# A two-stage classifier contraction: the transposed operand made by crossbar DMAs instead of GpSimd products

## What is computed

```
variables = [softmax(p) for p in split(logits, 4, axis=-1)]     # four of 512 x 16: v0, v1, v2, v3
joint = outer product of the four, per row b                    # 512 x 16 x 16 x 16 x 16
flat = joint.reshape(512, 65536)
num_y_joint = einsum('bj,by->yj', flat, y_true)
num_joint = sum(flat, axis=0)
prob = clip(max(num_y_joint, 1e-6) / max(num_joint, 1e-6), 0, 1)
probs = einsum('yj,bj->by', prob, flat)                         # 512 x 100
```

## Time and profile before

| | |
|---|---|
| device time, median of 3 runs (lowest, highest) | 584.12 us (584.08, 584.28) |
| span of the profiled execution | 582.4 us |
| median less that span | 1.7 us |
| TensorE busy | 539.0 us, 93% |
| VectorE busy | 345.8 us, 59% |
| GpSimd busy | 135.8 us, 23% |
| ScalarE busy | 55.7 us, 10% |
| moved by DMA | 4.57 MB |

### The profile page before, as it was taken

One profiled execution on the slowest core, in us unless ns is written; L12 is line 12 of the kernel. 1 busy time (PEld: TensorE's weight loads), 2 busy tenths in 40 slices (PEclk: granted clock), 3 DMA queues, 4 the chain that ended last, 5 costly groups with the idle time before them and its releaser, 6 DMA issues.

```text
span 582.4 us, 10067 instructions
## 1 busy us (share of the span) xinstructions
PE 539.0 (93%) x3088; PEld 302.5 (52%) x3088; DVE 345.8 (59%) x735; ACT 55.7 (10%) x119; POOL 135.8 (23%) x96
## 2 busy tenths in 40 slices
PE   4777887579999999999999999999999999999996
PEld 2343443235555555555555555555555555555553
DVE  7899999996673644444454644445354644445445
ACT  4445454000001000000001000000001000000000
POOL 4899999990001300000001300000001300000000
PEclk9999998988999999999999999999999999999999
DMA  2111110000000000000000000000000000000000
GB/s 75 42 54 37 54 36 0 0 0 0 0 0 1 1 0 0 0 0 0 0 0 0 0 0 0 0 0 0 0 0 0 0 0 1 0 0 0 0 0 14
DMA packets 3013, 4.57 MB, mean 8 GB/s; under 512 B 816, under 2 KB 1072, under 8 KB 3008
## 3 DMA queue, kind: packets, MB, share of 16 engines
q1 hardware_dynamic: 2480, 4.30, 2.3%
q10 hardware_dynamic: 528, 0.20, 0.1%
HBM read 4.27 MB, written 0.24 MB: 8 GB/s over the span
## 4 chain that ended last, share of the span: by engine, by line
PE 77%; DVE 16%; issue 4%; DVEq 1%; ACT 1%; DMA 0%; POOL 0%; ACTq 0%; POOLq 0%
PE numbers L442 13%; PE numbers L443 13%; PE numbers L444 13%; PE joined L452 12%; PE joined L454 12%; PE joined L453 12%; DVE p_lo L351 9%; DVE r_hi L371 2%; DVE ratio L366 2%; DVEq L351 1%; DVE acc L406 1%; DVE inv L364 1%; ACT p_hi L281 0%; DVE qf L188 0%; DVE den L361 0%
## 5 line engine op out<-in xcount | busy, mean ns | idle before, releaser
L442 PE MATMUL numbers<-q_hi,p_hi 128*128 128x404 f16 (+1 forms) x508 | 172.7, 340 | 22.2 <-DVE p_lo L351 22.2
L452 PE MATMUL joined<-r_hi,pt_hi 128*128 128x400 f16 x512 | 170.9, 334 | 7.8 <-DVE r_lo L373 7.7
L443 PE MATMUL numbers<-q_lo,p_hi 128*128 128x404 f16 (+1 forms) x508 | 171.9, 338 | 0.0
L444 PE MATMUL numbers<-q_hi,p_lo 128*128 128x404 f16 (+1 forms) x508 | 171.8, 338 | 0.0
L453 PE MATMUL joined<-r_lo,pt_hi 128*128 128x400 f16 x512 | 170.7, 333 | 0.0
L454 PE MATMUL joined<-r_hi,pt_lo 128*128 128x400 f16 x512 | 170.5, 333 | 0.0
L361 DVE TENSOR_SCALAR den<-numbers 128x4 f32<-128x4 f32 x128 | 20.5, 160 | 211.2 <-PE numbers L444 209.9
L373 DVE SCALAR_TENSOR_TENSOR r_lo<-ratio,r_hi 128x400 f16<-128x400 f32 x128 | 99.5, 778 | 4.4
L442 PEld LDWEIGHTS numbers<-q_hi,p_hi 128*128 (+1 forms) x508 | 50.0, 98 | 63.7 <-issue 28.0
L258 POOL TENSOR_TENSOR qg<-qf,v0f 128x1600 f32<-128x1600 f32 x3 | 8.6, 2862 | 303.6 <-ACT qf L313 303.6
L452 PEld LDWEIGHTS joined<-r_hi,pt_hi 128*128 (+1 forms) x512 | 50.0, 98 | 50.4 <-issue 14.3
(11 more groups left out here) (53 smaller groups left out, 115.2 us busy)
## 6 DMA issues: line engine op xcount, KB each, us to landing
v1b<-v_rows SPq DMA_DIRECT2D x15, 256.0 KB, 3.2
labels<-in_r_y_true_dram ACTq DMA_DIRECT2D x1, 200.0 KB, 2.9
out_dram<-acc SPq DMA_DIRECT2D x1, 200.0 KB, 2.0
x<-in_r_logits_dram SPq DMA_DIRECT2D x1, 128.0 KB, 2.2
v_rows<-v1t SPq DMA_DIRECT2D x1, 32.0 KB, 1.6
```

What stands on the lines that cost most here:

```text
L442: pe.matmul(out, hi, qh, start=(k == 0), stop=False)
L443: pe.matmul(out, hi, ql, start=False, stop=False)
L444: last = pe.matmul(out, lo, qh, start=False, stop=(k == KC - 1))
L452: pe.matmul(out, hi, r_hi[:, slot, :], start=first, stop=False)
```

## The change

pt_hi and pt_lo are no longer computed from a transposed p23. They are copies of p_hi and p_lo whose 128 x 128 blocks are transposed on the way by `dma_start_transpose` on SP's queue, an instruction for hi and one for lo: one tile each for tiles 0 and 1, then two tiles (256 KB) for each value from 1 on. Four semaphores take turns, so that SP issues value i only when value i - 4 has landed. Removed are v1's way over DRAM, v1b, p23t, ptf, the identity matrix, all fp32 transposes of TensorE and the PSUM bank `spare`, ScalarE's copies of these, its pt_hi, and GpSimd's ptf and pt_lo. ScalarE's loop is now p_hi alone. GpSimd now begins q of groups 1 to 3 when all of p_lo is made (`p_ready` at TILES). On TensorE group 0's loop is written out value by value, since it waits on the four semaphores in turn. The unchanged parts are groups 1 to 3 and VectorE's program.

SP's queue:

```diff
-            sp.wait_ge(v1_copied, 1)
-            sp.dma_start(v1_dram, v1t[:, :]).then_inc(v1_stored, 16)
-            sp.wait_ge(v1_stored, 16)
-            for i in range(1, V1_BUFS):
-                sp.dma_start(v1b[:, i, :], v1_dram[i:i + 1, :].broadcast_to([LANES, ROWS])).then_inc(v1_spread[i], 16)
-
-            sp.wait_ge(ptf_made, 2)
-            sp.dma_start(v1b[:, 0, :],
-                         v1_dram[V1_BUFS:V1_BUFS + 1, :].broadcast_to([LANES, ROWS])).then_inc(v1_spread[0], 16)
-            def refill(i, buf):
-
-                sp.wait_ge(ptf_made, 2 * i + 2 * (1 - V1_BUFS))
-                sp.dma_start(v1b[:, buf, :],
-                             v1_dram[bass.ds(i, 1), :].broadcast_to([LANES, ROWS])).then_inc(v1_spread[buf], 16)
-
-            with sp.Fori(V1_BUFS, S - 2 * V1_BUFS + 1, V1_BUFS) as i:
-                for j in range(1, V1_BUFS + 1):
-                    refill(i + j, j % V1_BUFS)
-            for i in range(S - V1_BUFS + 1, S):
-                refill(i, i % V1_BUFS)
+            def turn(out, src, tile, tiles):
+                return sp.dma_start_transpose(
+                    out[:, bass.ds(tile * TW, tiles * TW)].rearrange("p (c b) -> p c b", b=LANES),
+                    src[:, bass.ds(tile * TW, tiles * TW)])
+
+            for h in range(2):
+                sp.wait_ge(p_hi_made, h + 1)
+                turn(pt_hi, p_hi, h, 1).then_inc(pt_hi_first[h], 16)
+                sp.wait_ge(p_ready, h + 1)
+                turn(pt_lo, p_lo, h, 1).then_inc(pt_lo_first[h], 16)
+
+            def turn_value(i, lap, j):
+
+                if lap is not None:
+                    sp.wait_ge(pt_landed[j], lap * 32)
+                sp.wait_ge(p_hi_made, 2 * i + 2)
+                turn(pt_hi, p_hi, 2 * i, 2).then_inc(pt_landed[j], 16)
+                sp.wait_ge(p_ready, 2 * i + 2)
+                turn(pt_lo, p_lo, 2 * i, 2).then_inc(pt_landed[j], 16)
+
+            for i in range(1, S):
+                turn_value(i, i // TURN_SEMS - (i % TURN_SEMS == 0) if i > TURN_SEMS else None, i % TURN_SEMS)
             sp.wait_ge(added, KC * AG)
```

GpSimd:

```diff
-            def make_pt(tile, half, buf, fill):
-
-                if half == 0 and fill is not None:
-                    pool.wait_ge(v1_spread[buf], fill)
-                if fill is not None:
-
-                    pool.wait_ge(pt_ready, tile - 1)
-                pool.tensor_tensor(ptf[:, half, :], p23t[:, half, :], v1b[:, buf, :], ALU.mult).then_inc(ptf_made, 1)
-
-            def finish_pt(tile, half):
-                pool.wait_ge(pt_hi_made, tile + 1)
-                pool.tensor_tensor(pt_lo[:, bass.ds(tile * TW, TW)], ptf[:, half, :],
-                                   pt_hi[:, bass.ds(tile * TW, TW)], ALU.subtract).then_inc(pt_ready, 1)
-
-            def make_value(i, buf, fill):
-                make_pt(2 * i, 0, buf, fill)
-                make_pt(2 * i + 1, 1, buf, fill)
-                finish_pt(2 * i, 0)
-                finish_pt(2 * i + 1, 1)
-
-
-            pool.wait_ge(v1_first_copied, 1)
-            pool.wait_ge(p23t_made, 1)
-            make_pt(0, 0, 0, None)
-            finish_pt(0, 0)
-            pool.wait_ge(p23t_made, 2)
-            make_pt(1, 1, 0, None)
-            finish_pt(1, 1)
-            for i in range(1, V1_BUFS):
-                make_value(i, i, 16)
-            with pool.Fori(V1_BUFS, S - V1_BUFS + 1, V1_BUFS) as i:
-                make_value(i, 0, i * (16 // V1_BUFS))
-                for j in range(1, V1_BUFS):
-                    make_value(i + j, j, (i + V1_BUFS) * (16 // V1_BUFS))
-
-
+            pool.wait_ge(p_ready, TILES)
```

ScalarE:

```diff
-            def make_pt_hi(tile, half):
-                act.wait_ge(ptf_made, tile + 1)
-                act.activation(pt_hi[:, bass.ds(tile * TW, TW)], ptf[:, half, :], ACT.Copy).then_inc(pt_hi_made, 1)
-
             act.wait_ge(p23_made, 1)
             make_p_hi(0, 0, 1)
             act.wait_ge(q0_right, 1)
             act.activation(q_hi[:, QH:QW], qf[:, QH:QW], ACT.Copy).then_inc(q0_right_hi, 1)
-            act.wait_ge(v1_turned, 1)
-            act.activation(v1t[:, :], v1_psum[0:S, 0:ROWS], ACT.Copy).then_inc(v1_copied, 1)
             act.wait_ge(p23_made, 2)
             make_p_hi(0, 1, 2)
-            act.wait_ge(v1_first_made, 1)
-            act.activation(v1b[:, 0, :], v1_first[:, 0:ROWS], ACT.Copy).then_inc(v1_first_copied, 1)
-            for h in range(2):
-                act.wait_ge(p23_turned, h + 1)
-                act.activation(p23t[:, h, :], turned[h][:, 0:ROWS], ACT.Copy).then_inc(p23t_made, 1)
-            make_pt_hi(0, 0)
             with act.Fori(1, S) as i:
                 make_p_hi(i, 0, 2)
-                make_pt_hi(2 * i - 1, 1)
-                make_pt_hi(2 * i, 0)
-            make_pt_hi(TILES - 1, 1)
```

TensorE (besides the transposes at the start, which are deleted):

```diff
-            pe.wait_ge(pt_ready, 1)
-            pe.wait_ge(v1_first_copied, 1)
-            pe.wait_ge(v1_copied, 1)
+            pe.wait_ge(pt_hi_first[0], 16)
+            pe.wait_ge(pt_lo_first[0], 16)
             join(0, 0, 0, first=True)
 
-            def middle(g, end, make=False):
+            def middle(g, end):
 
                 with pe.Fori(1, end) as i:
-                    if make:
-
-                        pe.wait_ge(p_ready, 2 * i + 2)
                     count(g, 2 * i, 0)
-                    if make:
-                        pe.wait_ge(pt_ready, 2 * i)
                     join(g, 2 * i - 1, 1)
                     count(g, 2 * i + 1, 1)
-                    if make:
-                        pe.wait_ge(pt_ready, 2 * i + 1)
                     join(g, 2 * i, 0)
+
+            def first_value(i, j, lap):
+
+                pe.wait_ge(p_ready, 2 * i + 2)
+                count(0, 2 * i, 0)
+                if j is None:
+                    pe.wait_ge(pt_hi_first[1], 16)
+                    pe.wait_ge(pt_lo_first[1], 16)
+                join(0, 2 * i - 1, 1)
+                count(0, 2 * i + 1, 1)
+                pe.wait_ge(pt_landed[i % TURN_SEMS], lap * 32)
+                join(0, 2 * i, 0)
...
-            middle(0, S, make=True)
-            pe.wait_ge(pt_ready, TILES)
+            first_value(1, None, 1)
+            for i in range(2, S):
+                first_value(i, i % TURN_SEMS, i // TURN_SEMS + (i % TURN_SEMS > 0))
```

More of the change, by code:

```diff
@@ L63, in sem @@
             return ctx.enter_context(nc.semaphore(name))
-        v1_dram = nc.dram_tensor("v1_rows", [S, ROWS], FP32, kind="Internal").ap()
         x = sb("x", [LANES, KC * NV, S], FP32)
@@ L72, in joint_classifier @@
         labels = sb("labels", [LANES, KC, CW], FP32)
-        ident = sb("ident", [LANES, LANES], FP32)
         p23 = sb("p23", [LANES, KC, 2 * HALF], FP32)
[L76 to L80, removed]
+        TURN_SEMS = 4
         p_hi = sb("p_hi", [LANES, TILES * TW], FP16)
@@ L103, in joint_classifier @@
         joined = [pb(f"joined{i}", [LANES, 512], FP32) for i in range(KC)]
[L104 to L108, removed]
         logits_in = sem("logits_in")
@@ L112, in joint_classifier @@
         ones_set = sem("ones_set")
-        ident_set = sem("ident_set")
         acc_set = sem("acc_set")
@@ L118, in joint_classifier @@
         soft = sem("soft")
[L119 to L124, removed]
         p23_made = sem("p23_made")
-        p23_turned = sem("p23_turned")
-        p23t_made = sem("p23t_made")
         q0_left = sem("q0_left")
@@ L137, in joint_classifier @@
         p_ready = sem("p_ready")
-        ptf_made = sem("ptf_made")
-        pt_hi_made = sem("pt_hi_made")
-        pt_ready = sem("pt_ready")
+        pt_hi_first = [sem(f"pt_hi_first{h}") for h in range(2)]
+        pt_lo_first = [sem(f"pt_lo_first{h}") for h in range(2)]
+        pt_landed = [sem(f"pt_landed{j}") for j in range(TURN_SEMS)]
         numbers_ready = sem("numbers_ready")
@@ L192, in _ @@
             pool.memset(labels[:, :, CLASSES:CW], 1.0).then_inc(ones_set, 1)
[L193 to L196, removed]
             pool.memset(acc[:, :, :], 0.0).then_inc(acc_set, 1)
@@ L411, in _ @@
         def _(pe):
[L412 to L420, removed]
-            last.then_inc(v1_first_made, 1)
-            def turn_p23(h):
-                pe.wait_ge(p23_made, h + 1)
-                for k in range(KC):
-                    last = pe.transpose(turned[h][:, k * LANES:(k + 1) * LANES],
-                                        p23[:, k, h * HALF:(h + 1) * HALF], ident[:, :])
-                last.then_inc(p23_turned, 1)
             def count_parts(g, tile, k):
@@ L467, in _ @@
             out = numbers[0][:, 0:NW]
-            turn_p23(0)
             pe.wait_ge(p_hi_made, 1)
@@ L473, in _ @@
                 if k == KC // 2:
-                    turn_p23(1)
                     pe.wait_ge(q0_right_hi, 1)
```

## The result

The changed kernel takes 548.34 us (median of 4 runs, 547.58 to 548.90), the kernel before 584.10 us on the same chip (4 runs); the ratio is 0.940, 95% interval 0.938 to 0.942. The forecast was 548.5 us. The profiled execution took 547.58 us and spans 545.8 us, where the sum gave 546.8 us.

A forecast was written before the change was run, and what follows sets the result against it. TensorE was taken to bound the kernel, except in group 0, where it waits for VectorE, held up by GpSimd. Span 582.4 - 40.6 + 1 + 4 = 546.8 us, 548.5 us as timed; range 542 to 610 us.

The forecast's parts named there:

- the sum: Whole span: profiled 582.4 us less 40.6, plus 1 and plus 4, gives 546.8 us of span, 548.5 us as timed.
- Two regimes, GpSimd the cause: Group 0: a value takes 12.42 us early, 8.17 us late; VectorE's instructions wait for gaps between GpSimd's.
- The rival that VectorE would stay slow: Group 0: p_lo slow for another reason, such as transposes' SBUF traffic; about 12 us a value, 580 to 590 us; chance 0.02.
- -40.6 us: Count 0 to count 20: GpSimd's 64 products leave group 0, so the loss of 40.6 us goes.
- The start, +1 us: Start: fp32 turns and ScalarE copies go; TensorE's clock may rise one count later, 0 to 2 us, taken as +1.
- q, +4 us: GpSimd's q of groups 1 to 3, after the last p_lo, delays VectorE's r_hi and r_lo: +4 us, bounds 0 and 6.
- The straight code, 0: TensorE's fifteen values written out: more program fetching, taken as 0; +10 us if half a dozen fetches showed.
- The transposes, hidden: Group 0: SP's two 256 KB transposes a value finish within 8.17 us and cost 0; chance 0.70, 548.5 us.
- the bound from below: Transposes in group 0: 0.52 MB a value at the SP queue's 0.32 MB/us take 1.6 us.
- The slower rival: Transposes bound group 0, costing (T - 8.17) x 15 more, T a value's two transposes; up to 810 us; chance 0.23.
- the upper bound: Transposes in group 0: blocks go one behind another, 16 at 1.6 us, 25.6 us a value, 810 us in all.

The follow-up runs named there:

- the run with the groups apart: Changed kernel with GpSimd's q of groups 2 and 3 moved apart, each made from the middle of the running group, nothing added: 547.07 us.
- both q edits: Changed kernel with GpSimd's q instructions of groups 1 to 3 cut into four and q of groups 2 and 3 moved apart: 544.00 us, ratio 0.933.
- q cut: Changed kernel with each of GpSimd's nine instructions for q of groups 1 to 3 cut into four, same place and order: 545.95 us, ratio 0.935.

## Why the prediction was right

- **Two regimes, GpSimd the cause.** Right, and shown by the run with GpSimd's work put back: a value takes 11.4 to 12.8 us again, with every other part of the change in place and nobody waiting for GpSimd. The total, 582.4 us against 583.4 us before, is as close as it is by chance: 7.3 us of it stand at the start, and the kernel before lost 14.3 us beside q instead. The rival that VectorE would stay slow is refuted by 1.67 us for four p_lo under transposes, and under four times as many.
- **-40.6 us.** Count 20 ended 40.45 us earlier. From count 0 to count 20 are 79.95 us where 39 pieces gave 79.6 us. The prediction puts the whole 40.6 us down to the products' leaving. By the starts of den, 25.9 us were lost beside the products and 14.3 us beside q, and these are gone because q now waits for the last p_lo: with q early again the time is 15.7 us longer.
- **The start, +1 us.** Count 0 ended at 15.50 us, 0.17 us earlier than before, and the clock rose at about 15.4 us: nothing was lost in this execution. In others something was (last section), inside the bounds of 0 to 2 us.
- **q, +4 us.** The number is right and its working is not, which is luck. The excess of the steps from 132.21 to 168.90 us is 4.03 us, but only 2.40 us of it stand beside q. The other 1.63 us stand beside the first sum, which follows right behind q now and has no term in the prediction; in the kernel before it stood alone, at 187.65 us, and cost 0.18 us. The step beside q was put at 5.26 us, less 2 us of slack; it is 4.4 to 4.7 us, 5.3 us only beside the first sum, and the slack does not help, as the run with the groups apart shows.
- **The straight code, 0.** TensorE is busy in all of 28 to 95 us, which is straight code.
- **The transposes, hidden.** Right in sign, with the bound from below too low: I had 1.6 us a value from the refills' 0.32 MB/us, and it is 2.8 us, by the most that SP issued and the engines moved, 184 GB/s. The landing, 3.2 us, was taken rightly from the refill. The Trainium skill (Advanced Engine Details and Errata, X-Bar Transpose) expects 350 to 400 GB/s; no run here shows it: the most is half of that, with the engines' busy share at 1.0 and SP's queue never idle. The verdict did not hang on it: 8.17 us were there for either.
- **The slower rival** was a real one, and what decides it is the number of instructions, not of blocks: 2 a value are 2.5 us of SP, 16 are 20.4 us. It would have been slower by SP's issue, not by blocks that go one behind another, as the upper bound had it. I had taken the case of large transposes for the reason that they look like refills; the better reason would have been that the cost of issue is paid once for each.

## To carry to other kernels

An engine at 23% busy can cost another its time: where a VectorE instruction lasts much longer in one stretch than in another, look at what GpSimd runs beside it, and cut GpSimd's instructions short if they cannot be moved. Before moving work to DMA transposes, count both the instructions by their issue time and the bytes by the engines' busy share, against the time of one loop; here 2.5 and 2.9 us (0.36 of 8.17 us) against 8.2 us. Slack before a wait is not a store: 2 us stood free in each step of VectorE, and a chain of 4.5 us or more in a step of 4.08 us was late from its first step on.

## What the hardware showed that I had not expected

- SP takes 1.2 to 1.3 us to issue a transpose of one, four or eight 128x128 blocks, and 1.4 us on average in a row of large ones, where a plain DMA of 256 KB took 0.33 us before.
- Transposes in fp16 run in packets of 256 bytes, and the 16 engines' busy share was 0.36 at 68 GB/s, 0.72 at 130 GB/s and 1.02 at 184 GB/s. By these shares full engines move 180 to 190 GB/s so, an estimate, since SP's queue was never idle at 184 GB/s either. The plain refills come to 0.32 MB/us by their share.
- Not every VectorE instruction waits out GpSimd's. p_lo and r_lo, with two inputs in SBUF, do, and r_hi, with one; inv (SBUF to SBUF, 0.18 us), den (0.16 us) and ratio (0.57 us), the last two reading PSUM, take the same time everywhere; inv and den are only 4 columns wide, so whether their size or their operands spare them is not shown. The Trainium skill (Advanced Engine Details and Errata, GPSIMD Details) has GpSimd share ports with VectorE and clash with instructions of two SBUF inputs or in a 2-port mode; the trace agrees for p_lo and r_lo, which end just after a GpSimd instruction has ended. GpSimd itself loses less: its qg took 2.90 to 3.18 us in the changed kernel and up to 3.34 us beside the early p_lo.
- The rise of TensorE's clock after the start is not at the same time in each execution. Matmuls of the first counts are 0.34 us apart (1.2 GHz) and then 0.17 us (2.4 GHz) from 15.5 us on in the profiled execution of the changed kernel, from 17.0 us on with both q edits, and from 18.2 us on with q cut, though the same work stands before. Count 2 ended at 21.93, 22.52 and 23.03 us, and between 21.91 and 23.29 us over the seven profiled executions in which TensorE does the same up to there. That is up to 1.4 us of the scatter between runs, and I cannot say what decides it.
